# Expert loop of the first mixture: filler matmuls taken out, and the second product alternating between the two experts of a pair

## The reference, cut to what matters

```python
xn = xf / rms * norm_weight
logits = xn @ router_weight.T + router_bias
probs = softmax(logits)
_, idx = top_k(logits.T, 64)                   # 64 tokens for each of 16 experts
xe = xn[idx]                                   # 16 x 64 x 128
h = gelu(einsum('ecd,efd->ecf', xe, fc1_weight) + fc1_bias)     # 16 x 64 x 512
y = einsum('ecf,edf->ecd', h, fc2_weight) + fc2_bias            # 16 x 64 x 128
output = zeros.at[idx].add(y * gates)          # then divided by the sum of the gates
```

## Time and profile before

| | |
|---|---|
| median of three runs | 703.16 us (701.92 to 704.52) |
| profiled execution: its own time | 705.27 us |
| profiled execution: span from first to last instruction | 703.5 us |
| mean granted TensorE clock | 0.86 of full |
| PE busy | 535.8 us (76%), 3940 matmul records |
| DVE busy | 380.8 us (54%) |
| ACT busy | 217.9 us (31%) |
| all fillers (line 383) | 91.9 us in 266 records |

### The profile page before, as it was taken

The page is one execution under the profiler, slowest core; times in us unless marked ns, Lnnn a source line. Parts: engine busy times, 40 slices in busy tenths (PEclk is TensorE's granted clock), DMA queues, the critical chain, the costliest instruction groups (busy, mean ns, idle before and its releaser), DMA issues. The chain is left out here.

```text
span 703.5 us, 10323 instructions
## 1 busy us (share of the span) xinstructions
PE 535.8 (76%) x3940; PEld 311.5 (44%) x3940; DVE 380.8 (54%) x799; ACT 217.9 (31%) x441; POOL 137.9 (20%) x174
## 2 busy tenths in 40 slices
PE   4629999989999997211899835776399998679994
PEld 2406765655656563100378712353134554323331
DVE  1366554675666771479834455345566752344464
ACT  2101554446455665010111004212015566022121
POOL 4282302422132300520000010006412100300000
PEclk9568999999999999555889987695559989789998
DMA  9311211111111100510000030000201100000000
GB/s 323 155 43 52 60 32 47 48 47 47 47 48 47 47 3 0 210 63 0 1 1 1 2 135 0 0 1 0 76 15 47 47 2 1 2 0 0 1 15 15
DMA packets 32401, 29.56 MB, mean 42 GB/s; under 512 B 2912, under 2 KB 31072, under 8 KB 31840
## 3 DMA queue, kind: packets, MB, share of 16 engines
q1 hardware_dynamic: 32352, 28.90, 13.2%
HBM read 15.52 MB, written 0.52 MB: 23 GB/s over the span
## 5 line engine op out<-in xcount | busy, mean ns | idle before, releaser
L804 DVE TENSOR_REDUCE nmax<-bank 128x2 f32<-128x512 f32 (+2 forms) x240 | 142.1, 624 | 105.3 <-PE bank L610 54.5
L722 ACT ACTIVATE arena<-bank 128x512 f32<-128x512 f32 (+2 forms) x256 | 128.3, 525 | 119.4 <-PE bank L631 48.0
L610 PE MATMUL bank<-arena 66*128 66x256 bf16 (+2 forms) x512 | 92.5, 270 | 29.6 <-DMA arena<-qkl 26.4
L383 PE MATMUL bank<-causal_qk,identb 128*128 128x512 bf16 x266 | 91.9, 442 | 13.1 <-PEq L844 8.6
L631 PE MATMUL bank<-arena 68*128 68x256 bf16 (+2 forms) x512 | 86.9, 257 | 8.7 <-ACT arena L722 6.0
L610 PEld LDWEIGHTS bank<-arena 66*128 66x128 bf16 x512 | 46.2, 102 | 60.0 <-DMA arena<-qkl 27.9
L662 PE MATMUL bank<-arena 128*32 128x256 f32 (+4 forms) x1088 | 60.9, 345 | 2.1 <-ACT arena L722 1.9
L631 PEld LDWEIGHTS bank<-arena 68*128 68x128 bf16 x512 | 46.0, 98 | 32.7 <-ACT arena L722 16.2
L383 PEld LDWEIGHTS bank<-causal_qk,identb 128*128 128x128 bf16 x266 | 27.6, 110 | 47.2 <-issue 28.1
L662 PEld LDWEIGHTS bank<-arena 128*32 128x32 f32 x1088 | 27.3, 110 | 23.6 <-issue 9.0
L1499 DVE TENSOR_TENSOR arena<-bank,arena 128x512 f32<-128x512 f32 x24 | 16.6, 691 | 32.0 <-ACT arena L1454 32.0
(11 more groups left out here) (274 smaller groups left out, 858.9 us busy)
## 6 DMA issues: line engine op xcount, KB each, us to landing
arena<-qkl SPq DMA_DIRECT2D x192, 64.0 KB
fcw<-in_fc1T SPq DMA_DIRECT2D x1, 4096.0 KB, 17.5
arena<-in_fc2T SPq DMA_DIRECT2D x1, 4096.0 KB, 14.7
fcw<-in_last SPq DMA_DIRECT2D x1, 2304.0 KB, 8.2
w<-in_w SPq DMA_DIRECT2D x1, 1216.0 KB, 6.2
rows<-in_rows SPq DMA_DIRECT2D x1, 704.0 KB, 7.6
xT<-in_xT SPq DMA_DIRECT2D x1, 512.0 KB, 3.6
x<-in_x SPq DMA_DIRECT2D x1, 512.0 KB
```

The costliest lines, as they stand in the source:

```text
L383: nc.tensor.matmul(bank[:, :], m.identb[:, :], m.causal_qk[:, 0:4, :], start=True, stop=True)
L610: ins = t.matmul(out[:, i, :], m.qstack[n % 3][0:66, h, qt * P:(qt + 1) * P], m.kstack[n % 3][0:66, h, k0:k1], start=(i == 0), stop=(j.kin ...
L722: s.activation(m.prob[h % 8][:, 0:w], ST[c % NST][:, 0:w], ACT.Exp).then_inc(exps, 1)
L804: v.tensor_reduce(m.nmax[n % 2][:, qt, h0:h0 + nh], MX[c % NMX][:, 0:nh * (k1 - k0)].rearrange("p (h k) -> p h k", h=nh), AX.X, ALU.max, n ...
```

## The change

The constant `F_EXPERT` and the three calls of `keep_warm` before, in and behind the expert loop go. In `second` the two loops change places, so that expert 0 and expert 1 of the pair take turns, one f32 matmul each; the sums, their order within each expert and the semaphore at the end are the same. In the new kernel the lines behind `F_EXPERT` move up.

```diff
-F_EXPERT = 1
 WARM = 8
...
             def second(r):
                 pe.wait_ge(h_act, r + 1)
-                for half in range(2):
-                    for f in range(FT):
+                for f in range(FT):
+                    for half in range(2):
                         ins = t.matmul(B[4 + r // 4][64 * half:64 * half + 64, (r % 4) * D:(r % 4 + 1) * D],
                                        hact[r % 2][:, half, f, :], fc2[:, 2 * r + half, f, :],
                                        start=(f == 0), stop=(f == FT - 1), skip_group_check=True)
                 ins.then_inc(y_mm, 1)
 
-            keep_warm(nc, m, B[7], 3 * WARM // 2)
             for r in range(PAIRS):
                 if r >= 2:
                     pe.wait_ge(h_in, r - 1)
                 for half in range(2):
-                    keep_warm(nc, m, B[7], F_EXPERT)
                     e = 2 * r + half
...
             second(PAIRS - 1)
 
-            keep_warm(nc, m, B[7], 3 * WARM // 2)
             pe.wait_ge(ygl_ready, 1)
```

## The result

The changed kernel took 719.76 us (median of four runs, 714.67 to 723.41), the kernel before 703.84 (four runs, 701.92 to 705.52): 1.022 times, 95% interval 1.015 to 1.029. The forecast was 717.2, in a range of 706 to 722. A second measurement beside the experiments gave 1.0175 (1.014 to 1.021).

The account below looks back on a forecast made before the run. The prediction took PE to set the pace of the expert loop. At half clock the loop ends 11.9 us later and line 1027 loses 2.2, together 14.1 us on the profiled execution: 717.2 us on the median, range 706 to 722.

Parts of the forecast that it names:

- I take it that the clock stays at half through the loop: Expert loop: without fillers before it, PE's clock stays at 0.50, so the loop takes 50 us and ends 11.9 later.
- the sum: Whole stage: 11.9 us for the loop plus 2.2 for the matmuls of line 1027 make 14.1 us later.
- the lower bound of 11.4: Expert loop at half clock: the least delay of its end, 11.4 us, in bounds reaching 14.7.
- the scatter: Line 1027 behind the loop, 192 bf16 matmuls: starts at half clock after an idle wait and loses 2.2 us.
- A busy PE alone doesn't bring the clock back here: Expert loop: unbroken PE work isn't enough for full clock, as 20.07 busy of 20.40 us elsewhere stayed at 0.50.
- No stretch like 350.60 to 355.7 is left in it: Entry of the expert loop: the twelve fillers, 5.1 us ahead of full clock, go, and nothing like them remains.
- the alternation: Second products in the loop: two experts taking turns overlap, 8 steps instead of 12, 0.44 us per pair at full clock.
- The fillers inside the loop: Expert loop: removing sixteen fillers gives back 0.44 us per pair, 3.5 us in all, at full clock.
- the rival of an early rise: Expert loop: the clock rises soon after 350.60 as before, giving 696.2 us, faster by 1%; chance 0.14.
- the missing entry fillers: Before the expert loop: without twelve fillers of 5.1 us at half clock, 2.6 us come back if the clock rises as before.
- The fillers behind the loop: Behind the expert loop: twelve fillers lie under PE's wait for DVE and cost nothing; without them line 1027 starts at half clock.
- The Trainium skill's rule: Expert loop: back-to-back matmuls are the warm case, so by this rule the change wins 7 us.

Follow-up runs that it names:

- experiment 7: New kernel with twelve extra f32 first-product matmuls ahead of the expert loop, results unused: 722.56 us, 1.023 of the kernel before.
- Experiment 3: New kernel, still without fillers, with the second product in the old order (one expert after the other): 704.46 us, 0.999 of the kernel before.
- Experiment 2: Kernel before with only the two loops of `second` swapped, all fillers kept: 702.15 us, 0.996 of the kernel before.
- experiments 9 and 11: New kernel with, in 9, two fillers behind each second product in the loop: 705.71 us; in 11, the first two second products in old order: 700.45 us.
- experiment 1: New kernel with the twelve fillers before the loop put back: 703.84 us, 0.995 of the kernel before.
- experiments 4 and 8: New kernel with twelve fillers behind the loop plus, in 4, twelve before it: 700.70 us; in 8, fourteen between broadcasts: 698.83 us over two groups.
- experiment 6: New kernel with the sixteen fillers in the loop put back, none before or behind it: 721.96 us, 1.018 of the kernel before.

## Why the prediction was right, step by step

**"I take it that the clock stays at half through the loop"** held in the traces of both measurements. Each part of the sum came out: a pair 6.47 us (6.43 forecast), the loop 11.4 us longer (11.9; the lower bound of 11.4 was the better value, the hand-overs between forms didn't double), the scatter 2.1 us longer (2.2). 13.6 us of stage against 14.1. The median moved by 15.9, with an interval from 1.015 to 1.029 that holds the 1.019 of the stage alone as well. In the profiled execution the rest lies in the attention, which the change leaves alone; in the trace of the second measurement, 1.0175, the third broadcast starts at 348.89, as early as before.

**"A busy PE alone doesn't bring the clock back here"** is shown by experiment 7.

**"No stretch like 350.60 to 355.7 is left in it"** was true and not the whole reason. It reads as if the missing fillers were the loss. Experiment 3 shows that without any filler, but in the old order, the stage is 0.2 us longer than before and the ratio 0.999: its own second product, 2.8 us at half clock, stood before a rise. Experiment 2 shows that the alternation alone gains. Only both together lose: the fillers go that gave the loop its clock, and the alternation shortens the one other stretch that gave it back, from 2.82 to 1.91 us. In the prediction the alternation stood as a gain in all cases. In the sum it was one (8 instead of 12 steps in a product); for the clock it is what decides, which experiments 9 and 11 show from two sides. So the forecast was right with some luck: the same reasoning put the kernel without fillers in the old order at 725.7 us, 21 too many, and it met the new kernel because that one happens to lack the longer product too.

**The fillers inside the loop** were sized wrong: 0.44 us per pair, measured 0.29, as each had covered a weight load. It didn't touch the forecast, but it did the rival of an early rise: experiment 1, whose loop is at full clock, has a stage 3.6 us shorter than before, and with the 2.6 us that the missing entry fillers were to give back it would be 6.2, not the 7.0 of that rival.

**The fillers behind the loop.** "They cost nothing now" was right. That the scatter before had full clock was true of its trace, and experiments 4 and 8 each have a trace in which the same twelve fillers didn't hold it.

**The Trainium skill's rule** ("TensorE: Matmul & The Clock Gate", section "Loop structure matters more than you think": back-to-back matmuls are the warm case) didn't hold for this loop: 49.4 us without a pause at 0.50 in the new kernel.

What stays open: why the clock rises behind 2.82 us of second product, or behind 1.91 us with two fillers, and behind 1.91 us with one filler only in the seventh pair (experiment 6). The lengths are what the traces show ahead of the rises; that length is what counts is argued, and experiment 6 and the end of the loop in experiment 7 (3.68 us of second products without a rise) speak against it as the whole rule. The short runs of experiment 6 were not traced. Why the attention has more half clock in one execution than in another, which moves the third broadcast by up to 8 us, wasn't looked into either.

## What to carry to other kernels

Two edits that each cost nothing or gain can lose together when one of them takes away the clock's help and the other the work that would have replaced it: read the granted clock of the stretch, and what PE did before each rise, before counting a shortened stream as a gain. In this kernel fillers paid under a wait that existed already, where they cost nothing (fourteen in 3.1 us), with a few more where the loop is thin: there each costs 0.2 us at full clock, against 0.43 for one at half clock on the path ahead of the loop. When single times fall into groups, compare stage lengths in the traces and not medians alone.

## What the runs showed of the hardware

- The first product goes at the pace of its 128x128 f32 weight loads: in the new kernel they fill 3.49 of the 3.61 us of sixteen records. A record takes 0.216 us at half clock (5.18 us for 24 in experiment 7) and 0.12 at full clock (1.93 us for 16 in experiment 1). PE was busy throughout the new kernel's loop, and the clock stood at 0.50 for 49.4 us.
- Two experts in the two column halves of the array run at the same time when they alternate: 1.09 us for sixteen records instead of 1.58 at full clock, 1.98 instead of 2.88 at half.
- A loop that holds 1.00 once it has it didn't reach it from 0.50 before its end: the same instructions ran at either level, 27 us in experiment 1 (356.71 to 383.98) and 49 us in the new kernel.
